# Attention and experts on one core: turning two batches' key values at a time, and ScalarE's second key eviction in two halves

## What is computed

```python
xn = layernorm(x)
q, k, v = heads(xn, Wq, bq), heads(xn, Wk, bk), heads(xn, Wv, bv)
qp = relu(einsum('bhsd,hdf->bhsf', q, rw)) + EPS
kp = relu(einsum('bhsd,hdf->bhsf', k, rw)) + EPS
kv = einsum('bhsf,bhsd->bhfd', kp, v)
qkv = einsum('bhsf,bhfd->bhsd', qp, kv)
norm = einsum('bhsf,bhf->bhs', qp, kp.sum(axis=2))
attn = (qkv / (norm + EPS)) @ Wo + bo
# experts: each row goes to its top one of 8
ffn = gate * (gelu(xn @ w1[e] + b1[e]) @ w2[e] + b2[e])
out = x + attn + ffn
```

## Time and profile before

| | |
|---|---|
| median of 3 runs | 204.85 us (204.78 to 205.59) |
| profiled execution | 203.99 us, span 201.9 us |
| TensorE busy | 93% of the span |
| VectorE, ScalarE, GpSimd busy | 67%, 66%, 60% |
| one attention iteration (5 to 14) | 5.06 us |
| granted TensorE clock, mean | 0.990 |

### The profile page before, as it was taken

How to read it: one execution, slowest core, us unless ns; L and a number is a source line. 1 busy time by engine, 2 the same in 40 slices (tenths; PEclk the granted TensorE clock), 3 DMA queues, 4 the chain that set the end, 5 groups by cost and what they waited for, 6 DMA issues and landing times. The chain is left out here.

```text
span 201.9 us, 6889 instructions
## 1 busy us (share of the span) xinstructions
PE 188.2 (93%) x2341; PEld 150.4 (74%) x2341; DVE 135.3 (67%) x469; ACT 132.9 (66%) x319; POOL 121.5 (60%) x156
## 2 busy tenths in 40 slices
PE   6779999999999999999999979999999999999960
PEld 6447677566666666666665658999999999999960
DVE  5898697587979777777777796555555555555540
ACT  3268869689777777777777664755655655655620
POOL 2069793111177666666664100887887888888884
PEclk9999999999999999999999999999999999999995
DMA  4830599999522212222248282898999999997330
GB/s 138 230 96 14 172 214 183 182 296 304 132 69 69 69 66 69 69 70 69 70 120 278 59 246 83 207 219 194 196 213 201 210 206 201 212 214 138 28 33 4
DMA packets 32464, 29.48 MB, mean 146 GB/s; under 512 B 5904, under 2 KB 24752, under 8 KB 32432
## 3 DMA queue, kind: packets, MB, share of 16 engines
q1 hardware_dynamic: 25792, 24.82, 46.5%
q0 software_dynamic: 6640, 4.24, 16.2%
HBM read 20.10 MB, written 11.49 MB: 156 GB/s over the span
## 5 line engine op out<-in xcount | busy, mean ns | idle before, releaser
L454 POOL DMA_INDIRECT out<-k_all,slots_all x39 | 60.9, 1562 | 24.5 <-DMA out<-res 11.9
L845 ACT ACTIVATE q_all<-feat,w_slot 128x128 f32<-128x128 f32 x156 | 44.5, 368 | 30.7 <-PE feat L683 30.7
L683 PE MATMUL feat<-v_all,w_slot 128*128 128x128 f32 x312 | 41.2, 275 | 0.0
L424 POOL DMA_INDIRECT sorted_x<-rows_all,place_i x32 | 31.5, 985 | 15.7 <-PE feat L566 8.8
L683 PEld LDWEIGHTS feat<-v_all,w_slot 128*128 128x128 f32 x312 | 38.0, 192 | 0.0
L419 POOL TENSOR_SCALAR o_bias<-kv_sum,den_eps 128x1 f32<-128x1 f32 x32 | 9.2, 288 | 25.6 <-DVE kv_T L1074 19.6
L695 PE MATMUL o_bank<-w_sb,q_all 128*128 x160 | 21.2, 276 | 0.1
L1129 DVE SCALAR_TENSOR_TENSOR gated_b<-b_all,slots_all,out_row 128x128 f32<-128x128 f32 x39 | 13.8, 353 | 10.1 <-issue 10.1
L695 PE MATMUL feat<-w_sb,q_all 128*128 x152 | 20.1, 275 | 0.0
L695 PEld LDWEIGHTS o_bank<-w_sb,q_all 128*128 128x128 f32 x160 | 19.4, 192 | 0.3 <-issue 0.3
L388 POOL TENSOR_SCALAR rows_all<-x_all,meanvar,rstd 128x128 f32<-128x128 f32 x16 | 13.0, 822 | 11.1 <-DVE rstd L889 11.1
(11 more groups left out here) (148 smaller groups left out, 319.4 us busy)
## 6 DMA issues: line engine op xcount, KB each, us to landing
w_slot<-w1x SPq DMA_DIRECT2D x39, 258.0 KB, 3.5
sorted_x<-ones_f SPq DMA_DIRECT2D x1, 2535.0 KB, 17.5
w1x<-in_w SPq DMA_DIRECT2D x1, 2048.0 KB, 23.7
out<-res SPq DMA_DIRECT2D x16, 128.0 KB, 2.2
x_all<-in_x SPq DMA_DIRECT2D x7, 256.0 KB, 4.0
slots_all<-sorted_x SPq DMA_DIRECT2D x23, 65.0 KB, 3.4
out<-k_all,slots_all POOLq DMA_INDIRECT x39, 4.8
slots_all<-sorted_x SPq DMA_DIRECT2D x1, 520.0 KB, 5.4
```

The lines of the kernel that those rows point to most:

```text
L424: pool.indirect_dma_start(sorted_x, bass.IndirectOffsetOnAxis(ap=place_i[:, t:t + 1], axis=0), rows_all[:, t, :], None).then_inc(x_moved, 16)
L454: pool.indirect_dma_start(out_rows, bass.IndirectOffsetOnAxis(ap=slot_rows[j % SLOT_RING][:, D + 1:XW].bitcast(I32), axis=0), y_sb[j % Y_R ...
L683: ins = pe.matmul(bank[:, a * P:(a + 1) * P], w1_slot[j % W1_RING][:, a * P:(a + 1) * P], xsT[j % X_RING][:, :], start=True, stop=True)
L845: act.activation(hidden_T[j % H_RING][:, a * P:(a + 1) * P], hid_bank[j % HID][:, a * P:(a + 1) * P], ACT.Gelu, bias=w1_slot[j % W1_RING][ ...
```

## The change

`turn` now takes a first and a last batch. In odd iterations it transposes two batches' key values (i - 2 and i - 1; in iteration 1 batch 0 alone), four transposes into 512 columns of `kv_bank`, and ScalarE copies them with one instruction into `ka_pair`, which holds both `ka` buffers side by side. Even iterations have no turn and no such copy. Batch 15 is turned alone behind the loop, as before. ScalarE's second key eviction (1024 columns) is cut in two halves (`k_relu_half`); from iteration 3 on the second half comes after the output copies and, in odd iterations, after the copy of the turned key values. The counts that the semaphores wait for follow (`K_PARTS`, `turns_at`, `turned_at`).

```diff
+        ka_pair = sb("ka_pair", [P, 2, S], F32)
+        ka = [ka_pair[:, n, :] for n in range(2)]
...
+        def turns_at(i):
+            return (i + 1) // 2
+        def turned_at(b):
+            return 1 + turns_at(b)
...
 def key_values(b):
-                pe.wait_ge(k_act, 2 * b + 2)
+                pe.wait_ge(k_act, K_PARTS * (b + 1))
                 pe.wait_ge(k_dve, b + 1)
-                due(pe, ka_ready, b)
+                due(pe, ka_ready, turns_at(b))
...
-            def turn(i):
-                due(pe, ka_ready, i - 1)
-                pe.wait_ge(kv_ready, 2 * i)
+            def turn(first, last):
+                pe.wait_ge(kv_ready, 2 * (last + 1))
...
+                for b in range(first, last + 1):
+                    for par in range(2):
+                        at = (b - first) * S + par * P
+                        ins = pe.transpose(bank[:, at:at + P], kv_T[b % 2][:, par, :], ident[:, :])
                 ins.then_inc(turn_ps, 1)
...
-                if i >= 1:
-                    turn(i)
+                if i % 2 == 1:
+                    turn(max(i - 2, 0), i - 1)
...
+            def k_relu_half(b, half):
+                at = (2 + half) * GH
+                act.activation(k_feat[b % 2][:, at:at + GH, 0:P],
+                               key_pair(b)[1][:, half * 512:(half + 1) * 512].rearrange("p (c n) -> p c n", n=P), ACT.Relu) \
                     .then_inc(k_act, 1)
...
+            def save_turned(first, last):
+                act.wait_ge(turn_ps, turned_at(last))
+                due(act, o_ps, last - 1)
+                n = last - first + 1
+                act.activation(ka_pair[:, 2 - n:2, :].rearrange("p n d -> p (n d)") if last < NBATCH - 1 else ka[0],
+                               (kv_ps_t if last < NBATCH - 1 else kt_bank)[:, 0:n * S], ACT.Copy).then_inc(ka_ready, 1)
...
                 k_relu(i)
+                if i < 3:
+                    k_relu_half(i, 1)
...
                 if i >= 3:
                     save_outputs(i - 3)
-                if i >= 1:
-                    save_turned(i)
+                if i % 2 == 1:
+                    save_turned(max(i - 2, 0), i - 1)
+                if i >= 3:
+                    k_relu_half(i, 1)
...
             def mask_kv(b):
-                due(dve, turn_ps, b - 1)
+                due(dve, turn_ps, turns_at(b))
```

More of the change, by code:

```diff
@@ L54 @@
 REGS = 3
+K_PARTS = 3
 NORM = [0, 0, 2, 2] + [3] * (CHUNKS - 4)
@@ L125, in build @@
         o_bias = [sb(f"o_bias{n}", [P, 2], F32) for n in range(3)]
-        ka = [sb(f"ka{n}", [P, S], F32) for n in range(2)]
+        ka_pair = sb("ka_pair", [P, 2, S], F32)
+        ka = [ka_pair[:, n, :] for n in range(2)]
         pk = [sb(f"pk{n}", [P, S // TB, 2, TB], F32) for n in range(2)]
@@ L539, in k_features @@
                 elif b > 1:
-                    pe.wait_ge(k_act, 2 * b)
+                    pe.wait_ge(k_act, K_PARTS * b)
                     pe.wait_ge(q_act, 2 * b - 3)
@@ L553, in q_features @@
                 if b < NBATCH - 1:
-                    pe.wait_ge(k_act, 2 * b + 3)
+                    pe.wait_ge(k_act, K_PARTS * (b + 1) + 1)
                     pe.wait_ge(k_dve, b + 2)
@@ L583, in key_values @@
                 ins.then_inc(kv_ps, 1)
-            def turn(i):
-                due(pe, ka_ready, i - 1)
-                pe.wait_ge(kv_ready, 2 * i)
-                if i == NBATCH:
+            def turn(first, last):
+                pe.wait_ge(kv_ready, 2 * (last + 1))
+                if last == NBATCH - 1:
                     pe.wait_ge(q_act, 2 * (NBATCH - 1))
-                for par in range(2):
-                    ins = pe.transpose((kv_ps_t if i < NBATCH else kt_bank)[:, par * P:(par + 1) * P], kv_T[(i - 1) % 2][:, par, :], ident[:, :])
+                bank = kv_ps_t if last < NBATCH - 1 else kt_bank
+                for b in range(first, last + 1):
+                    for par in range(2):
+                        at = (b - first) * S + par * P
+                        ins = pe.transpose(bank[:, at:at + P], kv_T[b % 2][:, par, :], ident[:, :])
                 ins.then_inc(turn_ps, 1)
@@ L595, in outputs @@
                 s = b % 2
-                pe.wait_ge(ka_ready, b + 1)
+                pe.wait_ge(ka_ready, turned_at(b))
                 pe.wait_ge(q_act, 2 * b + 2)
@@ L702, in _ @@
             q_features(15)
-            turn(16)
+            turn(15, 15)
             out_project(12)
@@ L785, in k_relu @@
                 due(act, kv_ps, b - 1)
-                first, second = key_pair(b)
-                act.activation(k_feat[s][:, 0:GH, 0:P], first[:, 0:512].rearrange("p (c n) -> p c n", n=P), ACT.Relu) \
+                act.activation(k_feat[s][:, 0:GH, 0:P], key_pair(b)[0][:, 0:512].rearrange("p (c n) -> p c n", n=P), ACT.Relu) \
                     .then_inc(k_act, 1)
-                act.activation(k_feat[s][:, 2 * GH:4 * GH, 0:P], second[:, :].rearrange("p (c n) -> p c n", n=P), ACT.Relu) \
+                k_relu_half(b, 0)
+            def k_relu_half(b, half):
+                at = (2 + half) * GH
+                act.activation(k_feat[b % 2][:, at:at + GH, 0:P],
+                               key_pair(b)[1][:, half * 512:(half + 1) * 512].rearrange("p (c n) -> p c n", n=P), ACT.Relu) \
                     .then_inc(k_act, 1)
@@ L853, in _ @@
             q_relu_first(15)
-            save_turned(16)
+            save_turned(15, 15)
             q_relu_second(15)
```

4 lines of the change are left out of this document (removed).

## The result

| | before | changed |
|---|---|---|
| median of 20 runs each, taken in turn | 205.4 us (204.4 to 206.1, and one run of 1038.41) | 206.47 us (205.3 to 207.49) |
| ratio, 95% interval | | 1.0057 [1.004, 1.0073] |
| profiled execution, span | 203.99 us, 201.9 us | 206.92 us, 204.9 us |
| granted TensorE clock, mean | 0.990 | 0.993 |

The account below looks back on a forecast made before the run. Bound read stage by stage: TensorE's timeline per attention iteration (5.06 us), experts following its shift. Terms -0.85 (pairs), +0.18 (iteration 15), +0.18 (start) sum to -0.49 us, 204.4 us on the median; range 203.3 to 205.4.

Parts of the forecast that it names:

- 0.12 us is what a ScalarE result needs to reach TensorE: Attention loop: travel time read where the out projection follows ScalarE's output copies, used also for key values' start.
- Even iterations: Attention loop without a turn: key values starts 0.10 us late behind ScalarE's last half, iteration 4.71 us instead of 5.06.
- Odd ones: Attention loop with four transposes: ScalarE's last half and TensorE tie at 4.15 us, iteration 5.24 us instead of 5.06.
- Pairs: Attention loop, iterations 5 to 14: 9.95 us a pair against 10.12, 0.17 saved each, 0.85 us for five.
- Iteration 15: Last iteration of the attention loop, odd and alone: 5.24 against 5.06 us, 0.18 lost.
- The start: Iterations 2 to 4: key values of iteration 3 wait 0.28 us longer; cost 0.18 us, bounds 0 and 0.28.
- Other work: VectorE's early copies and query eviction, GpSimd's moves shifting with the loop, dropped met waits: given nothing.
- a shift of its start passes to the end: Expert stage, not edited: an earlier or later start moves the kernel's end, if the attention loop's end shifts.
- Rival B: Waits for nothing visible in iterations 4 and 15 go away, 1.09 us more saved, 203.3 us; chance 0.17.
- Rival C: Attention loop: even iterations wait 0.30 us instead of 0.10, pairs gain nothing, about 205.2 us; chance 0.11.
- Rival D: Attention loop: overlap of ScalarE's instructions is lost where it waits, slower, 206.1 us; chance 0.12.
- A: Whole kernel as forecast: 204.4 us, between 203.9 and 204.8; chance 0.60.

Follow-up runs that it names:

- e1: Changed kernel with key_values' wait for ScalarE's keys written first, so the first matmul carries it: 204.25 us, 0.9943 of before.
- e9: Changed kernel without key_values' wait for ScalarE's value copies from batch 8 on, one wait instruction less: 205.29 us, 1.0024 of before.
- e5: Changed kernel with four more waits per batch in key_values from batch 3 on, all met long before: 209.34 us, 1.0195 of before.
- e10: The changed kernel unedited, measured again beside the other runs: 207.04 us, 1.0109 of before.
- e6: e1 with pairs turned in even iterations and batches 14 and 15 turned together behind the loop: 205.17 us, 1.0006 of before.
- e12: The program of e6, unedited, measured again: 204.8 us, 0.9985 of before.
- e2: Kernel before with key_values' wait for ScalarE's keys moved onto the first matmul: 205.0 us, 0.9993 of before.
- e8: Kernel before with out_project's wait for ScalarE's output copies moved onto the first matmul: 204.58 us, 0.9946 of before.

## Why the prediction was wrong, point by point

*The step that failed first* is "0.12 us is what a ScalarE result needs to reach TensorE". The number was right for the out projection, with one wait instruction ahead of its matmul, and was carried over to the key values, which have two and then three. In "TensorE may start the key values at 3.66" the 0.12 is 0.18 and then 0.33. Distances measured, from the end of ScalarE's instruction to the load, by the wait instructions from the one with the late condition to the matmul:

| wait instructions | 0 | 1 | 2 | 3 | 4 | 5 |
|---|---|---|---|---|---|---|
| distance, us | 0.05 (e1) | 0.12 (before) | 0.18 (change, e9) | 0.33 (change) | 0.39 (e5) | 0.54 (e5) |

*Even iterations*, 4.71 forecast: 4.78 and then 4.92. *Odd ones*, 5.24: 5.25 and then 5.41; the tie at 4.15 left no room for the 0.21. *Pairs*: 9.95 forecast, 10.04 and 10.33 measured (one of 10.43), so the term of -0.85 came out +0.70. With the wait on the matmul (e1) the pair of 9.85 is even below the forecast. *Iteration 15*, +0.18: the same cause makes it 5.41 (key values at 113.32, 4.36 behind the key features, and 1.05 from there), +0.35.

*The start*, +0.18: right but for a hole. TensorE in iterations 3 and 4 of the changed kernel, answering to the earlier trace rows, and below it the load of iteration 3 before (the 49.77 of the earlier trace rows is its matmul):

```profile
50.71 0.85 PEld L591 LDWEIGHTS kv_bank<-k_feat,v_all 128*32 128x32 f32 x32 [0.80 <-issue]
51.76 0.74 PEld L558 LDWEIGHTS feat<-rw_bd,k_all 32*128 32x128 f32 x16 [0.20 <-issue]
...
54.15 0.34 PEld L576 LDWEIGHTS feat<-q_all,rw_bd 32*128 32x128 f32 x7 [0.73 <-ACT k_feat L804]
55.24 0.61 PEld L576 LDWEIGHTS feat<-q_all,rw_bd 32*128 32x128 f32 x9 [0.76 <-issue]
```

```profile
49.74 0.85 PEld L581 LDWEIGHTS kv_bank<-k_feat,v_all 128*32 128x32 f32 x32 [0.66 <-issue]
```

Key values wait until 4.20 behind their key features instead of 3.84, 0.36 later where 0.28 was reckoned with; the query features of iteration 4 come 2.39 behind theirs instead of 2.54, which gives 0.15 back: 0.21 net. Then 0.76 us pass inside the query features, released by nothing.

*Other work*, "I give these edits nothing", and "a shift of its start passes to the end": this is the second step that failed. The shift passed, and 1.04 us came on top. The earlier trace rows and the 11.93 us that GpSimd waits ahead of its first transfer stood in the trace before; how little the 1.56 us of a transfer and the 0.30 behind it leave of a slot's 1.90 was not read from it. What was lost is measured; that the code packet is its cause is the untested reading above.

*Rival B* was half right. The hole near 111 is gone from the change, but the one in iteration 4 grew from 0.28 to 0.76. The second trace of the same program, e10, has it in the same place and longer:

```profile
55.28 0.61 PEld L576 LDWEIGHTS feat<-q_all,rw_bd 32*128 32x128 f32 x9 [1.03 <-issue]
```

In e6 it is 1.29 and in e12, the same program, 1.57; a hole of 0.79 in iteration 2 stands in e6 alone. In e2, which has before's order of work, iterations 2 and 4 take 5.94 and 6.04 us, where before's profile has 5.38 and 5.38. So the holes can grow as well as go, and one execution of a program doesn't fix their length. A q8 packet of code moves 1 to 2 us ahead of each one in iteration 4 (at 52.6 for the hole at 54.5 in the change); many such packets have no hole behind them, and that they are the cause isn't shown. The Trainium skill (Runtime: NRT & Kernel Launch, section Instruction fetch mechanics) calls the cost of such a block mostly hidden. If the reading of the last write is right, six traces here disagree: the work behind a write that the block met came 1.5 to 2.0 us later.

*Rival C*, an even iteration's wait of 0.30 where 0.10 was forecast, describes the loop from iteration 8 on; "read from a wait that may not have been one" was the right doubt, and it wasn't followed to the list of instructions.

*Rival D* had sign and size, 206.1 against 206.47, by luck, for its mechanism is wrong and 1.04 us of the measured loss is on GpSimd: the overlap of ScalarE's instructions isn't lost, as the ends at 3.54 and 4.03 show. So is the estimate by the Trainium skill (ScalarE: Activation LUTs, section What ACT_TABLE_LOAD costs) near the result for another reason: by it the halves would have ended 0.13 and 0.16 later than they did.

What was right: outputs to query features 1.00 in even iterations and 1.58 in odd ones (forecast 1.59), the copies at 2.2, the whole order on ScalarE. The rule given in advance, "if odd ones wait visibly: then ScalarE's path is longer than I read it", pointed at the right place; the length is on TensorE's side of it. A slip in the sum of chances changes nothing: B and a tenth of A make 0.23, not 0.25.

## What to carry to other kernels

Before a condition becomes the last one to be met, look at where its wait stands: put the wait that is met last on the matmul itself and the met ones ahead of it. Here that one moved line takes the change from 1.0057 to 0.9943 of before (e1), and gives the kernel before 0.9946 without any of the change (e8). A travel time read at one wait holds for that wait's place alone. And where an engine ends the program at a pace within 2% of what feeds it, most of a late start is still there at the end: here 1.04 of 1.7 us after 39 transfers.

## What the runs showed of the hardware

- A wait instruction whose condition is met costs nothing ahead of the late one (with one, two or three of them there, in e8 and e1, 0.05 to 0.07 us from ScalarE's end to the load in all iterations but one), and 0.06 to 0.15 us behind it; the profile calls this time "issue".
- Where one packet of program code (0.02 MB) moved in the middle of a write of 144 packets, 9 of these moved about 1 us behind the others, and the first work behind the write started 1.5 to 2.0 us later. Seen in six traces of six, and not tested by an edit of its own.
- TensorE shows holes of 0.2 to 1.57 us that nothing in the profile ends. Two traces of one program have most of them in the same places with different lengths (0.76 and 1.03, 1.29 and 1.57 us); one of 0.79 us was in one trace of two.
- GpSimd's transfer of 128 rows with an add into DRAM takes 1.56 us (up to 1.60 in part of the change's), with 0.30 to the next.
